# New step orders for the five engines of a batched attention kernel with adaptive normalization

## The chip, the cores and the metric

The kernel runs on one core of one Trainium2 chip. The metric is the device time of one launch in microseconds (us), as the median of several runs. A profile of one execution was taken beside the runs.

## The reference

```
scale, shift = split(emb @ W_emb + b_emb)              # emb: one row of 1024 for each batch
xn  = rms_norm(x, g_norm) * (1 + scale) + shift        # x: (8, 512, 1024)
q, k, v = xn @ W_qkv                                   # 16 heads of 64
q, k = rms_norm(q, g_q), rms_norm(k, g_k)
attn = softmax(q k^T * 64**-0.5)
o = attn @ v                                           # back to (8, 512, 1024)
out = x + o + o @ W_out
```

All data are float32.

## The kernel before

Every large product is made in two parts: an operand is split into a rounded high part (`_hi`, on ScalarE) and the rest (`_lo`, on VectorE or GpSimd), and TensorE multiplies high by high, high by low and low by high. The first two matmuls of a product keep the high part of the activations (L500, L501), the third has the low one (L502). The weights are split once, in the first batch, kept in `w_store` in HBM, and loaded again for each later batch.

The work is cut into *steps*, and each engine has its own written list of steps for the first batch (`HEAD`), for each of the six batches in the middle (`BODY`, run six times) and for the last one (`TAIL`). A step is written as pair of heads, letter, number: `7W0` is step W0 of pair 7. A batch has eight pairs. The lists run over the borders of a batch: a cycle of `BODY` begins with pair 2 of its own batch, and `8` and `9` are pairs 0 and 1 of the next. The letters, with the engines in the order in which the work passes them:

- **C** (TensorE, 4 for each of 4 tiles of 128 rows, six matmuls each): projection of q, k and v of a pair into `proj_bank`. **D** (ScalarE copies v and squares q and k, VectorE sums, GpSimd takes the root in two operations, L970 and L973) and **M** (VectorE, q and k scaled into `qk_stage`) drain the tile; two tiles later the bank is used again.
- **T** (TensorE turns q (T0) or k (T1) with four transposes into a `flip_bank`; ScalarE makes the high part, VectorE the low one).
- **S** (TensorE, scores of 128 queries by 512 keys into a `score_bank`; VectorE takes the maximum, L859; ScalarE the exponential with the row sum, L718). There are two score banks: S(n+2) waits for the exponential of S(n). **N** (VectorE): reciprocal of the row sum, L863, and the scaling of `probs`, L865, an operation with input and output in SBUF.
- **F** (TensorE turns 512 columns of `probs` with four transposes, L598, into one of two `flip_bank`s; ScalarE writes `pt_hi`, L724; VectorE `pt_lo`, L869, which frees the bank). **W** (TensorE, L609 and L610, product with v) needs both. F0 and F4 wait for the four N before them.
- **O** (ScalarE, VectorE: the two parts of the output added), **Q** (ScalarE `o_hi`, L734; GpSimd `o_lo`, L966, which reads and writes SBUF), **V** (ScalarE, GpSimd: parts of v), **P** (TensorE, output projection, 48 for a batch) and **R** (VectorE adds the residual, which a DMA brought).
- **A**, **X** (the next batch's x: square and scale, turn, modulate, split; the lows of X on GpSimd, L960), **L** (weights split in the first batch, on ScalarE, VectorE L767 and GpSimd L933), **B**.

Each engine runs its list strictly in order, and every step waits on semaphores for what it needs. So an order never changes what is computed, only who waits for whom. In `flip_places` and `flip_at` the places of T, F and X in TensorE's list say which of the two flip banks and which semaphore counts they use. The two waits that the prediction speaks of most:

```python
pe.wait_ge(exp_done, it * 8 + (n - 2 + 1 + CREDIT))                  # S
pe.wait_ge(flip_free, flip_at(order, b, "F", n, p)[0] + 1)           # W
```

Of the kernel before, what the change touches and what calls it, by code (L numbers as in the profile page):

```python
# [35 lines left out]
        X0 Z0 X1 0C0 0C1 0C2 X2 0C3 0C4 0C5 0C6 X3 0C7 0C8 0C9 0C10 0C11 0C12 0C13 0C14 0C15 1C0 1C1 1C2 1C3 0T0 0T1 1C4  # L36
        1C5 1C6 1C7 1C8 1C9 0S0 0S1 1C10 1C11 0S2 0S3 1C12 1C13 0S4 0S5 1C14 0F0 0F1 1C15 0S6 0S7 2C0 0F2 0F3 0W0 0W1
        2C1 2C2 0W2 2C3 0W3 1T0 1T1 2C4 2C5 2C6 2C7 0F4 2C8 2C9 0F5 1S0 0F6 0W4 1S1 2C10 0F7 0W5 1S2 1S3 0W6 2C11 0W7
        2C12 1S4 1S5 1F0 1F1 2C13 2C14 1F2 1W0 1F3 1W1 1S6 1S7 1W2 2C15 1W3 3C0 3C1 1F4 1F5 3C2 3C3 2T0 2T1 1W4 1W5 3C4
        3C5 3C6 1F6 3C7 3C8 1F7 1W6 2S0 2S1 3C9 3C10 1W7 2S2 3C11 3C12 2S3 2S4 3C13 3C14 3C15 2S5 2S6 4C0 2F0 2F1 4C1  # L40
        4C2 2S7 4C3 3T0 3T1 2W0 2W1 4C4 4C5 2F2 4C6 4C7 4C8 2F3 2W2 3S0 2F4 3S1 2F5 2W3 4C9 3S2 2F6 2W4 3S3 2F7 2W5 4C10
        2W6 4C11 2W7 3S4 3S5 4C12 3F0 3F1 4C13 3S6 4C14 3F2 3W0 3F3 3W1 3S7 4C15 3W2 5C0 3W3 3F4 3F5 5C1 5C2 3F6 3F7 3W4
        3W5 5C3 5C4 4T0 4T1 3W6 3W7 5C5 5C6 5C7 5C8 5C9 4S0 4S1 5C10 5C11 4S2 4S3 5C12 5C13 4S4 4S5 5C14 4F0 4F1 5C15
        4S6 4S7 6C0 4F2 4F3 4W0 4W1 6C1 6C2 5T0 4W2 5T1 4W3 6C3 6C4 6C5 4F4 6C6 6C7 6C8 4F5 5S0 4F6 4W4 5S1 6C9 4F7 4W5
# [40 lines left out]
        X1 1L0 1L1 1L2 X3 1L3 0D0 X5 0D1 X7 0D2 0D3 2L0 2L1 2L2 2L3 1D0 0V0 0V1 1D1 1D2 3L0 1D3 3L1 3L2 3L3 2D0 1V0 2D1
        1V1 2D2 0Q0 2D3 4L0 4L1 2V0 4L2 4L3 3D0 +A0 3D1 +A1 +A2 +A3 2V1 3D2 1Q0 5L0 3D3 5L1 5L2 5L3 4D0 4D1 3V0 3V1 4D2
        2Q0 6L0 4D3 6L1 6L2 6L3 4V0 5D0 4V1 5D1 3Q0 5D2 7L0 5D3 7L1 7L2 7L3 5V0 6D0 6D1 5V1 4Q0 6D2 6D3 6V0 7D0 +X0 +X1
        7D1 7D2 +X2 +X3 6V1 7D3 +X4 +X5 5Q0 8D0 +X6 +X7 8D1 8D2 7V0 7V1 8D3 L0 L1 L2 L3 6Q0 9D0 8V0 9D1 9D2 8V1 7Q0 9D3
        L4 L5 L6 L7 9V0 9V1 L8 L9 L10 L11""".split(),
# [1061 lines left out]
```

## Time and profile before

| | |
|---|---|
| median of 3 runs (lowest, highest) | 2278.11 us (2276.98, 2279.11) |
| profiled execution: its own time | 2278.89 us |
| profiled execution: span of its instructions | 2276.0 us |
| mean granted TensorE clock | 0.999 |
| TensorE, VectorE, ScalarE, GpSimd busy | 2256.2, 1597.9, 1345.7, 651.7 us |

The profile gives for each instruction the engine, the line, the start and the duration. TensorE's matmuls are pipelined: one is shown as lasting until its end is drained, while the next has begun. What a matmul costs TensorE is therefore the distance from its start to the next one's start, not its duration. TensorE can also be held up by less than the length of one matmul without an idle time being shown.

### The profile page before, as it was taken

The page shows a single profiled execution, that of the slowest core. Times are in us where ns is not written, and L with a number is a line of the kernel's source. Part 1 is how long each engine was busy: PE and PEld are TensorE (multiplying, and loading weights), DVE is VectorE, ACT ScalarE, POOL GpSimd, SP SyncE. Part 2 cuts the span into 40 slices and gives each one's busy share as a digit, 9 for nine tenths or more (in the row PEclk, how much of TensorE's full clock was granted, in tenths as well). Part 3 has the DMA queues.
Part 4 walks back from the last instruction along what each step waited for, and adds up shares of the span by engine and source line. Part 5 has one row for each costly group of instructions (what it writes and reads, how often), then busy time and mean ns, then how long its engine had stood idle before and what let it go on. Part 6 is the DMA issues. An engine that isn't in the chain of part 4 may idle for free.

```text
span 2276.0 us, 36733 instructions
## 1 busy us (share of the span) xinstructions
PE 2256.2 (99%) x13392; PEld 2110.3 (93%) x13392; DVE 1597.9 (70%) x3284; ACT 1345.7 (59%) x3101; POOL 651.7 (29%) x880
## 2 busy tenths in 40 slices
...
DMA packets 71269, 346.35 MB, mean 152 GB/s; under 512 B 7601, under 2 KB 43441, under 8 KB 47537
## 3 DMA queue, kind: packets, MB, share of 16 engines
...
## 4 chain that ended last, share of the span: by engine, by line
PE 86%; DVE 8%; ACT 2%; issue 1%; POOL 0%; DMA 0%; ACTq 0%; DVEq 0%
PE proj_bank L502 18%; PE proj_bank L500 18%; PE proj_bank L501 18%; PE flip_bank L598 9%; PE pv_bank L609 5%; PE pv_bank L610 5%; PE score_bank L590 4%; PE score_bank L591 4%; PE flip_bank L553 2%; DVE probs L865 2%; DVE neg_max L859 2%; DVE pt_lo L869 2%; PE flip_bank L563 1%; ACT k_hi L700 1%; PE proj_bank L525 1%
## 5 line engine op out<-in xcount | busy, mean ns | idle before, releaser
L500 PE MATMUL proj_bank<-w_split,xn_hi 128*128 128x384 f32 x2048 | 700.0, 342 | 1.4 <-DVE res L907 0.8
L502 PE MATMUL proj_bank<-w_split,xn_lo 128*128 128x384 f32 x2048 | 688.5, 336 | 0.0
L501 PE MATMUL proj_bank<-w_split,xn_hi 128*128 128x384 f32 x2048 | 687.4, 336 | 0.0
L718 ACT ACTIVATE probs<-score_bank,neg_max 128x512 f32<-128x512 f32 x512 | 352.6, 691 | 213.5 <-DVE neg_max L859 211.2
L500 PEld LDWEIGHTS proj_bank<-w_split,xn_hi 128*128 128x128 f32 x2048 | 385.2, 188 | 18.1 <-DVE xn_lo L854 1.0
L501 PEld LDWEIGHTS proj_bank<-w_split,xn_hi 128*128 128x128 f32 x2048 | 385.5, 188 | 15.2
L724 ACT CAST pt_hi<-flip_bank 128x512 fp32r<-128x512 f32 x512 | 288.8, 591 | 182.0 <-PE flip_bank L598 91.1
L869 DVE TENSOR_TENSOR pt_lo<-flip_bank,pt_hi 128x512 fp32r<-128x512 f32 x512 | 339.9, 685 | 78.1 <-ACT pt_hi L724 75.9
L502 PEld LDWEIGHTS proj_bank<-w_split,xn_lo 128*128 128x128 f32 x2048 | 384.8, 188 | 0.0
L859 DVE TENSOR_REDUCE neg_max<-score_bank 128x1 f32<-128x512 f32 x512 | 341.3, 684 | 17.0 <-PE score_bank L591 13.0
L865 DVE TENSOR_SCALAR probs<-probs,row_inv 128x512 f32<-128x512 f32 x512 | 275.7, 539 | 18.1
L598 PE MATMUL flip_bank<-ident,probs 128*128 128x128 f32 x2048 | 284.4, 273 | 1.1 <-DVE q_split L830 0.4
L598 PEld LDWEIGHTS flip_bank<-ident,probs 128*128 128x128 f32 x2048 | 242.5, 140 | 32.8 <-DVE pt_lo L869 7.3
L973 POOL TENSOR_TENSOR qk_rstd<-qk_ms_eps,neg_half 128x4 f32<-128x4 f32 x256 | 264.6, 1033 | 20.0
L970 POOL TENSOR_TENSOR qk_ms_eps<-qk_ms,eps_col 128x4 f32<-128x4 f32 x256 | 55.3, 216 | 719.2 <-DVE qk_ms L880 719.1
L609 PE MATMUL pv_bank<-pt_hi,v_split 128*128 128x512 f32 x512 | 224.3, 438 | 4.2 <-DVE pt_lo L869 4.2
L500 PE MATMUL proj_bank<-w_split,o_hi 128*128 128x384 f32 (+1 forms) x672 | 215.2, 320 | 0.0
L951 POOL TENSOR_TENSOR v_split<-v_stage,v_split 128x256 fp32r<-128x256 f32 x128 | 98.9, 773 | 401.3 <-ACT v_split L688 401.3
L502 PE MATMUL proj_bank<-w_split,o_lo 128*128 128x384 f32 (+1 forms) x672 | 213.6, 318 | 0.0
L501 PE MATMUL proj_bank<-w_split,o_hi 128*128 128x384 f32 (+1 forms) x672 | 213.5, 318 | 0.0
L590 PE MATMUL score_bank<-k_hi,q_split 128*128 128x512 f32 x512 | 206.0, 402 | 0.1
L591 PE MATMUL score_bank<-k_lo,q_split 128*128 128x512 f32 x512 | 201.6, 394 | 0.0
...
## 6 DMA issues: line engine op xcount, KB each, us to landing
...
```

Source lines behind the costliest of these rows:

```text
L500: nc.tensor.matmul(dst, a_hi, w_hi, start=(kt == 0), stop=False)
L501: nc.tensor.matmul(dst, a_hi, w_lo, start=False, stop=False)
L502: mm = nc.tensor.matmul(dst, a_lo, w_hi, start=False, stop=(kt == KT - 1))
L590: nc.tensor.matmul(score_bank[n % 2][:, :], q_t, k_hi[h][:, :], start=True, stop=False)
L591: nc.tensor.matmul(score_bank[n % 2][:, :], q_t, k_lo[h][:, :], start=False, stop=True).then_inc(score_full, 1)
L598: mm = nc.tensor.transpose(flip_bank[flip][:, qt * P:(qt + 1) * P], probs[h][:, qt, i * P:(i + 1) * P], ident[:, :])
L609: nc.tensor.matmul(pv_bank[h][:, :], v_t, pt_hi[n % 2][:, :], start=(i == 0), stop=False)
L718: nc.scalar.activation(probs[h][:, i, :], score_bank[n % 2][:, :], ACT.Exp, bias=neg_max[:, n:n + 1], accum_out=row_sum[:, n:n + 1]).then_ ...
L724: nc.scalar.copy(pt_hi[n % 2][:, :], flip_bank[flip][:, :]).then_inc(flip_hi, 1)
L859: nc.vector.tensor_reduce(neg_max[:, n:n + 1], score_bank[n % 2][:, :], AX.X, ALU.max, negate=True).then_inc(max_done, 1)
L865: nc.vector.tensor_scalar(probs[h][:, i, :], probs[h][:, i, :], row_inv[:, n:n + 1], None, ALU.mult).then_inc(probs_ready, 1)
L869: nc.vector.tensor_tensor(pt_lo[n % 2][:, :], flip_bank[flip][:, :], f32(pt_hi[n % 2][:, :]), ALU.subtract).then_inc(flip_free, 1)
```

## The change

It puts other step orders in the place of the old ones for all five engines, in `HEAD`, `BODY` and `TAIL`. Each list has the same steps as before. No function, wait, buffer or operation is edited. Of SyncE's lists only one pair of steps in `BODY` is exchanged (`E8 W4` becomes `W4 E8`); `HEAD` and `TAIL` have the same SyncE order as before. Shown are the lines of which the prediction speaks. The places of T, F and X in TensorE's list move, and with them the flip bank that a step uses.

```diff
--- before.py
+++ after.py
@@ -33,60 +33,60 @@
 HEAD = {
     "TensorE": """
...
-        7S1 6F3 6W1 6F4 6W2 8C12 7S2 6F5 6W3 7S3 6F6 6W4 8C13 6F7 6W5 7S4 6W6 8C14 8C15 6W7 7S5 7F0 7F1 7S6 9C0 9C1 7F2
-        8T0 7W0 7W1 7S7 9C2 9C3 8T1 7W2 9C4 7F3 9C5 9C6 9C7 8S0 8S1 7W3 9C8 7F4 7F5 9C9 8S2 9C10 8S3 9C11 7F6 7F7 7W4
...
+        6F5 7S0 7S1 6W4 8C10 6F6 6F7 6W5 7S2 8C11 7S3 +X3 6W6 6W7 7S4 7S5 7F0 7F1 7S6 7W0 7F2 7S7 7W1 7F3 8C12 8C13 7W2
+        7F4 7F5 7W3 8C14 7F6 7W4 7W5 7F7 8C15 9C0 7W6 9C1 7W7 8T0 9C2 9C3 8T1 9C4 9C5 9C6 9C7 8S0 8S1 9C8 9C9 8S2 8S3
...
     "VectorE": """
...
-        7N0 6F4 7N1 7S2 6F5 6O0 6F6 7N2 7S3 6F7 7S4 7N3 7N4 8D3 7S5 6O1 7F0 7F1 8M3 L0 7N5 L1 L2 L3 7F2 7S6 8T0 9D0 7S7
...
+        6F6 8D1 6F7 7S2 7S3 +X3 7N2 7S4 7N3 7S5 8M1 6O1 7F0 7N4 7F1 7S6 7N5 7S7 7F2 7N6 7N7 7F3 7F4 8D2 7F5 7F6 8M2 8D3
...
@@ -96,84 +96,84 @@
 BODY = {
     "TensorE": """
...
-        3F0 3F1 4C13 4C14 3F2 3W0 3F3 3W1 3S6 3S7 3W2 4C15 3W3 5C0 5C1 3F4 3F5 5C2 5C3 4T0 4T1 3W4 3W5 5C4 5C5 3F6 5C6
...
-        6F5 6W3 7S3 6F6 6W4 8C13 6F7 6W5 7S4 6W6 8C14 8C15 6W7 7S5 7F0 7F1 7S6 9C0 9C1 7F2 8T0 7W0 7W1 7S7 9C2 9C3 8T1
...
-        8S6 8F0 8F1 9C14 9C15 8F2 8F3 8W0 8W1 8S7 P0 8W2 8W3 9T0 9T1 P1 P2 P3 P4 8F4 P5 P6 8F5 8F6 8W4 9S0 9S1 8F7 8W5
...
+        3S6 3F0 2W6 2W7 4C15 3S7 3F1 5C0 5C1 3F2 3W0 3F3 3W1 5C2 3F4 3W2 3W3 5C3 3F5 3W4 4T0 5C4 4T1 5C5 5C6 5C7 3F6 5C8
...
+        7S3 +X3 6W6 7S4 6W7 7S5 8C10 8C11 7F0 7F1 7S6 7S7 7W0 7F2 7W1 7F3 8C12 8C13 8C14 8C15 7W2 9C0 7F4 7F5 7W3 9C1
+        7W4 7F6 7F7 7W5 9C2 8T0 9C3 9C4 7W6 8T1 9C5 7W7 9C6 9C7 9C8 9C9 8S0 8S1 9C10 9C11 8S2 8S3 9C12 9C13 9C14 8S4 8S5
+        8F0 9C15 8F1 P0 8S6 8S7 8W0 8F2 P1 8F3 8W1 9T0 P2 P3 9T1 P4 P5 8W2 P6 8F4 P7 8W3 8F5 8W4 8F6 9S0 9S1 P8 P9 P10
...
     "ScalarE": """
...
-        2F2 2F3 4D0 3T0 3V0 3T1 4D1 2F4 2O0 2F5 3S0 2F6 3S1 2F7 3S2 3S3 4D2 3V1 2O1 3F0 3S4 3F1 3S5 2Q0 3F2 3F3 3S6 4D3
...
+        4D0 3T0 3T1 2F4 +A3 3V0 4D1 3S0 3S1 2F5 2O0 1Q0 3S2 2F6 4D2 2F7 3S3 3S4 3S5 3S6 3V1 3F0 2O1 4D3 3F1 3S7 3F2 3F3
+        2Q0 3F4 3F5 5D0 4T0 4T1 5D1 3F6 3F7 4S0 4S1 4S2 4S3 5D2 4V0 3O0 4F0 4S4 4S5 4F1 5D3 3O1 4F2 4F3 4S6 4S7 4V1 4F4
...
     "VectorE": """
...
-        2F6 3N1 2F7 3S2 3S3 3N2 3N3 4D2 3S4 2O1 3S5 3F0 4M2 3F1 3N4 3N5 3F2 3S6 3F3 3S7 3N6 4D3 3N7 3O0 4M3 3F4 3F5 5D0
...
-        8N4 8S5 8S6 8F0 8F1 8N5 8N6 9D3 8F2 8F3 9M3 8S7 8N7 9T0 R0 9T1 8F4 8O0 8F5 9S0 8F6 9S1 9N0 R1 8F7 9N1 9S2 9S3
...
+        3S3 2F6 4D2 3N2 2F7 3S4 2O0 3N3 4M2 3S5 3S6 3N4 3N5 3F0 3S7 4D3 3F1 2O1 3N6 3N7 3F2 3F3 4M3 3F4 3F5 5D0 5M0 4T0
...
+        6F4 6O0 6F5 7S0 7S1 6F6 7N0 6F7 7S2 7S3 +X3 7S4 7N1 7N2 7N3 7S5 8D1 7F0 7F1 8M1 7S6 7S7 7F2 8D2 7N4 7N5 8M2 7N6
+        7N7 6O1 7F3 8D3 7F4 8M3 7F5 7F6 7F7 9D0 9M0 8T0 8T1 9D1 8S0 8S1 9M1 8N0 8S2 8S3 7O0 8N1 9D2 8N2 8N3 9M2 8S4 8S5
+        8F0 8N4 9D3 7O1 8F1 9M3 8F2 8S6 8S7 8F3 8N5 R0 8N6 9T0 8N7 9T1 8F4 R1 8F5 8F6 9S0 9N0 9S1 9S2 9S3 9N1 9N2 R2 8F7
...
     "GpSimd": """
-        0Q0 1Q0 2D0 2D1 2D2 2V0 2D3 2V1 3D0 3D1 +A0 +A1 3D2 +A2 +A3 3D3 4D0 3V0 4D1 3V1 4D2 2Q0 4D3 4V0 5D0 5D1 4V1 3Q0
-        5D2 5D3 5V0 6D0 6D1 5V1 4Q0 6D2 6D3 6V0 7D0 +X0 +X1 7D1 7D2 +X2 +X3 6V1 7D3 +X4 +X5 5Q0 8D0 +X6 +X7 8D1 8D2 7V0
-        7V1 8D3 6Q0 9D0 9D1 8V0 8V1 9D2 7Q0 9D3 9V0 9V1""".split(),
+        0Q0 2D0 2D1 2D2 2D3 3D0 3D1 3D2 2V0 2V1 +A0 +A1 +A2 3D3 4D0 4D1 1Q0 4D2 3V0 3V1 4D3 5D0 +A3 2Q0 5D1 4V0 5D2 5D3
+        4V1 6D0 6D1 3Q0 5V0 5V1 6D2 6D3 7D0 7D1 6V0 +X0 +X1 4Q0 7D2 +X2 6V1 +X3 7D3 8D0 +X4 +X5 5Q0 7V0 +X6 8D1 +X7 7V1
+        8D2 8D3 6Q0 9D0 9D1 8V0 9D2 9D3 7Q0 8V1 9V0 9V1""".split(),
     "SyncE": """
-        E2 E3 E4 3W1 E5 4W0 4W1 +X0 +X1 +X2 +X3 5W0 5W1 6W0 6W1 7W0 7W1 8W0 8W1 9W0 9W1 W0 W1 W2 W3 O0 E6 O1 E7 O2 E8 W4
+        E2 E3 E4 3W1 E5 4W0 4W1 +X0 +X1 +X2 +X3 5W0 5W1 6W0 6W1 7W0 7W1 8W0 8W1 9W0 9W1 W0 W1 W2 W3 O0 E6 O1 E7 O2 W4 E8
         W5 O3 E9 O4 E10 O5 E11 O6 10W0 +E0 10W1 O7 O8 O9 O10 11W0 +E1 O11""".split(),
 }
 
```

## Rows read from the trace of the kernel before

**Rows 1.** The page: busy time of each engine, share of the span, instructions

```profile
PE 2256.2 (99%) x13392; PEld 2110.3 (93%) x13392; DVE 1597.9 (70%) x3284; ACT 1345.7 (59%) x3101; POOL 651.7 (29%) x880
```

**Rows 2.** Busy time (count) in stretches, then the clock: first batch, a middle one

```profile
44.00:386.00 342.00, 338.03 (x2010) 316.30 (x2008) 274.73 (x549) 236.03 (x552) 138.33 (x166) 1.00 0.47 175
...
943.00:1222.00 279.00, 278.32 (x1671) 263.48 (x1670) 193.34 (x402) 163.33 (x376) 75.30 (x104) 1.00 0.39 144
```

**Rows 3.** Timeline, fourth batch, around 3W2: start, us, engine, line, [idle before]

```profile
1009.38 1.58 DVE L865 TENSOR_SCALAR probs<-probs,row_inv 128x512 f32<-128x512 f32 x1
1009.38 1.29 POOL L966 TENSOR_TENSOR o_lo<-o_pair,o_hi 128x512 fp32r<-128x512 f32 x1 [2.10 <-ACT o_hi L734]
...
1010.97 0.40 PE L590 MATMUL score_bank<-k_hi,q_split 128*128 128x512 f32 x1
1011.06 0.49 DVE L865 TENSOR_SCALAR probs<-probs,row_inv 128x512 f32<-128x512 f32 x1
1011.20 0.40 PE L591 MATMUL score_bank<-k_lo,q_split 128*128 128x512 f32 x1
1011.46 0.68 DVE L869 TENSOR_TENSOR pt_lo<-flip_bank,pt_hi 128x512 fp32r<-128x512 f32 x1
1012.06 0.68 DVE L859 TENSOR_REDUCE neg_max<-score_bank 128x1 f32<-128x512 f32 x1
1012.20 0.50 PE L609 MATMUL pv_bank<-pt_hi,v_split 128*128 128x512 f32 x1 [0.60 <-DVE pt_lo L869]
1012.53 0.39 PE L610 MATMUL pv_bank<-pt_lo,v_split 128*128 128x512 f32 x1
```

**Rows 4.** Timeline: the way of 3F4 and 3F5 with nothing queued

```profile
1016.38 1.03 PE L598 MATMUL flip_bank<-ident,probs 128*128 128x128 f32 x8
...
1017.01 1.08 ACT L724 CAST pt_hi<-flip_bank 128x512 fp32r<-128x512 f32 x2 [0.82 <-PE flip_bank L598]
1017.17 0.42 PE L500 MATMUL proj_bank<-w_split,xn_hi 128*128 128x384 f32 x1
...
1017.63 0.69 DVE L869 TENSOR_TENSOR pt_lo<-flip_bank,pt_hi 128x512 fp32r<-128x512 f32 x1 [0.39 <-ACT pt_hi L724]
```

**Rows 5.** Timeline, fourth batch, around 8F2

```profile
1155.12 1.02 DVE L865 TENSOR_SCALAR probs<-probs,row_inv 128x512 f32<-128x512 f32 x1
...
1157.56 0.34 PE L502 MATMUL proj_bank<-w_split,xn_lo 128*128 128x384 f32 x1
...
1157.98 1.25 PE L598 MATMUL flip_bank<-ident,probs 128*128 128x128 f32 x8
...
1158.99 0.47 PE L609 MATMUL pv_bank<-pt_hi,v_split 128*128 128x512 f32 x1
```

**Rows 6.** Timeline of TensorE, first batch, before 8T1

```profile
296.66 0.33 PE L501 MATMUL proj_bank<-w_split,xn_hi 128*128 128x384 f32 x1
296.83 0.34 PE L502 MATMUL proj_bank<-w_split,xn_lo 128*128 128x384 f32 x1
298.65 0.33 PE L553 MATMUL flip_bank<-ident,qk_stage 128*128 128x128 f32 x1 [1.48 <-DVE pt_lo L869]
```

**Rows 7.** Groups by line: VectorE's scaling of probs; count, busy us, mean ns, idle before

```profile
L865 DVE TENSOR_SCALAR probs<-probs,row_inv 128x512 f32<-128x512 f32 x512 | 275.7, 539 | 18.1
```

**Rows 8.** Timeline: an S step with nothing queued behind it

```profile
1151.06 0.40 PE L591 MATMUL score_bank<-k_lo,q_split 128*128 128x512 f32 x1
...
1151.50 0.69 DVE L859 TENSOR_REDUCE neg_max<-score_bank 128x1 f32<-128x512 f32 x1 [0.46 <-PE score_bank L591]
...
1152.81 0.19 ACT L718 ACTIVATION_READ_ACCUMULATOR probs<-score_bank,neg_max 128x1 f32 x1
```

**Rows 9.** Timeline: a T1 step on ScalarE and VectorE

```profile
1047.97 2.78 ACT L700 ACTIVATE k_hi<-flip_bank,gk_col 64x512 fp32r<-64x512 f32 x4
...
1050.78 1.51 DVE L834 SCALAR_TENSOR_TENSOR k_lo<-flip_bank,gk_col,k_hi 64x512 fp32r<-64x512 f32 x2 [1.49 <-ACT k_hi L700]
```

**Rows 10.** Groups by line: VectorE's part of X, four instructions a step

```profile
L796 DVE TENSOR_SCALAR y_half<-flip_bank,mod_now 128x128 f32<-128x128 f32 x128 | 43.7, 404 | 13.5 <-issue 8.2 <-PE flip_bank L563 4.4
```

More of the change, by code:

```diff
@@ L35 @@
     "TensorE": """
[L36 to L44, printed above, removed]
@@ L84 @@
-    "GpSimd": """
[L85 to L89, printed above, removed]
+        X0 Z0 X1 0C0 0C1 0C2 0C3 X2 0C4 0C5 0C6 0C7 X3 0C8 0C9 0C10 0C11 0C12 0C13 0C14 0C15 1C0 1C1 1C2 1C3 0T0 1C4 0T1
@@ new lines @@
+        1C5 1C6 1C7 1C8 1C9 0S0 1C10 0S1 1C11 0S2 1C12 0S3 1C13 1C14 1C15 0S4 0F0 0S5 0F1 2C0 2C1 0W0 0S6 0S7 0W1 0F2
+        0F3 2C2 2C3 1T0 1T1 2C4 2C5 0W2 2C6 2C7 2C8 0F4 0W3 1S0 0F5 1S1 2C9 0W4 1S2 0F6 1S3 0W5 0F7 2C10 2C11 1S4 0W6
+        0W7 2C12 1S5 1F0 1F1 2C13 2C14 2C15 1S6 1S7 1F2 1W0 1W1 3C0 1F3 3C1 3C2 2T0 3C3 2T1 1W2 3C4 3C5 1W3 3C6 1F4 3C7
+        2S0 2S1 1F5 3C8 3C9 1W4 1W5 2S2 1F6 1F7 3C10 3C11 2S3 1W6 3C12 2S4 3C13 2F0 2F1 1W7 2S5 3C14 3C15 4C0 2S6 2F2
+        2F3 2S7 2W0 2W1 4C1 4C2 3T0 4C3 3T1 4C4 2W2 4C5 2F4 2W3 4C6 4C7 2F5 2F6 3S0 3S1 2W4 2W5 2F7 4C8 4C9 3S2 3S3 4C10
@@ new lines @@
+        P22 9F0 9F1 P23 9S7 P24 P25 9W0 P26 P27 9F2 9F3 P28 P29 P30 9W1 P31 P32 P33 P34 P35 P36 P37 9F4 9W2 9W3 9F5 P38
+        P39 P40 9F6 P41 P42 9F7 9W4 9W5 P43 P44 P45 9W6 P46 9W7 P47""".split(),
+    "ScalarE": """
+        X0 Y0 Y1 1L0 1L1 X1 Y2 Y3 0D0 1L2 X2 Y4 Y5 1L3 0D1 X3 Y6 Y7 0D2 0D3 0V0 0V1 2L0 2L1 1D0 0T0 0T1 2L2 2L3 1D1 0S0
+        0S1 0S2 1D2 0S3 3L0 1D3 0F0 0F1 0S4 0S5 3L1 0S6 0F2 0F3 3L2 2D0 0S7 1T0 1T1 3L3 0F4 2D1 0F5 1S0 1S1 1S2 0F6 0F7
+        0O0 2D2 1S3 1S4 0O1 1F0 1F1 1V0 1V1 1S5 2D3 4L0 4L1 4L2 1F2 1F3 1S6 1S7 2T0 3D0 2T1 4L3 1O0 1F4 2V0 +A0 +A1 1F5
+        3D1 2S0 0Q0 2S1 1F6 1F7 3D2 2S2 2S3 +A2 +A3 2F0 2F1 1O1 2S4 2S5 2V1 3D3 5L0 5L1 5L2 5L3 2F2 2F3 2S6 2S7 3T0 3T1
+        2F4 4D0 3V0 1Q0 4D1 2F5 2O0 2F6 3S0 2F7 3S1 3S2 3S3 4D2 3V1 2O1 3F0 3S4 3S5 3F1 2Q0 3F2 3S6 3F3 3S7 4D3 3O0 4V0
+        3F4 3F5 6L0 6L1 3F6 4T0 6L2 5D0 4T1 5D1 3F7 4S0 4S1 4S2 4S3 6L3 5D2 4F0 4S4 4F1 3O1 4S5 4S6 4F2 4S7 4F3 4V1 5D3
+        7L0 7L1 7L2 4F4 7L3 4F5 6D0 5T0 5T1 4F6 6D1 3Q0 5V0 5S0 5S1 4F7 5S2 4O0 5S3 6D2 5S4 5F0 5F1 4O1 5V1 6D3 5S5 5F2
+        5F3 5S6 6T0 5S7 6T1 5F4 6V0 4Q0 7D0 7D1 5O0 +X0 5F5 6S0 6S1 5F6 5F7 6S2 6S3 +X1 6S4 6F0 6F1 5O1 7D2 7D3 6S5 6V1
+        6F2 6F3 6S6 5Q0 6S7 7V0 +X2 8D0 7T0 7T1 6F4 6O0 6F5 8D1 7S0 7S1 6F6 6F7 8D2 7S2 7S3 6O1 +X3 7F0 7S4 7F1 7S5 7F2
+        7S6 7S7 7F3 6Q0 7F4 7V1 7F5 7F6 7F7 7O0 8D3 L0 L1 8V0 L2 L3 8T0 9D0 8T1 8V1 7O1 9D1 8S0 8S1 8S2 8S3 8S4 8S5 7Q0
+        9D2 8F0 8F1 9D3 8S6 8S7 L4 8F2 8F3 8F4 8F5 L5 L6 9V0 9T0 9T1 8F6 8O0 L7 9S0 9S1 9S2 9S3 9S4 L8 L9 8F7 9S5 L10
+        L11 8O1 9V1 9F0 9F1 9S6 9S7 9F2 9F3 9F4 9F5 9F6 9F7 9O0 9O1""".split(),
```

169 lines of the change are left out of this document (81 added, 88 removed).

## The prediction, made before the change was run

> **What bounds the kernel now.** I read the page first. TensorE is busy 99% of the span, VectorE 70%, ScalarE 59% [rows 1], and its clock is full. A busy share can hide short waits, so I took stretches next: TensorE shows 4.0 us without a matmul in the 342 us of the first batch and 0.7 in the 279 of a middle one, both at clock 1.00 [rows 2]. Then the waits by name: what TensorE waits for is nearly always VectorE, late with `pt_lo` [rows 3]. As a matmul overlaps the next one, I read the real price of a wait in the timeline, from start to start.
>
> From those distances come the prices of a step. A matmul of S or W takes 0.23 us (1010.97 to 1011.20 [rows 3]), a step of two 0.46. Eight transposes and the drain behind them take 0.87 (1016.38 to 1017.17, and the next matmul 0.25 instead of 0.17 [rows 4]), so a step F or T takes 0.44, X twice that. A C step is six matmuls at 0.17 to 0.18 each (296.66 to 296.83 [rows 6]), 1.04 us. No list has a step more or less than before, so this work stays. What a new order can take away is waits alone.
>
> Adding up all distances that are longer than these prices gives some 20 us for the whole kernel. About 3 of them lie before 44 us, where x of the first batch is made ready; they stay. Some 7.5 lie in the first batch, 1.5 in each middle batch (9 in all), 0.3 in the last one. The largest of a middle batch are shown: before 3W2, where 1011.20 to 1012.20 is 1.00 instead of 0.23 and the next distance 0.33 instead of 0.23, so 0.87 lost [rows 3]; and before 8F2, where 1157.56 to 1157.98 is 0.42 instead of 0.17 and the eight transposes after it take 1.01 instead of 0.79, so 0.47 lost [rows 5]. The remaining 0.2, at 6F3 and 6S5, are of the same reading. The largest of the first batch is before 8T1: 296.83 to 298.65 is 1.82 instead of 0.17, 1.65 lost [rows 6].
>
> **The change part by part: what it removes.** Before 3W2 the reader sees why VectorE is late. Its scaling of 3N4 starts at 1009.38, together with GpSimd's `o_lo` of 2Q0, and takes 1.58 us where 0.49 is usual. All that follows, 3N5 and the `pt_lo` of 3F2, is 1.09 late [rows 3]. The line takes 275.7 us for its 512 [rows 7]; at 0.49 each it would be 251: 25 us of VectorE go to such meetings. 8N4 before 8F2 is another, 1.02 us [rows 5]. I looked at the stretch of each long one: a middle batch has six, 3N4, 5N2, 7N5 and 8N4 beside a Q, 6N0 and 6N2 beside the lows of x.
>
> The Trainium skill, page "SBUF — State Buffer", section "SBUF: two separate sides", says why: VectorE and GpSimd share a pair of ports, whichever instruction starts first holds it to its end, and the other is blocked; it counts operations of VectorE that use both read ports. The trace agrees: L865 waits, while `pt_lo`, which reads PSUM, keeps its 0.68 us. By that rule an N step beside a Q costs up to one Q, 1.29 us, more; with no rule at all I would only carry the 25 us over to the new lists, whatever their order.
>
> So I asked of each Q in the new `BODY` what stands beside it on VectorE. 2Q0 follows +A3 on GpSimd, and ScalarE makes its high part after 3F3: VectorE then has 4M3 3F4 3F5 5D0 5M0 4T0 4T1, no N. 6Q0 follows 8D3: 7F4 8M3 7F5 7F6 7F7, no N. 7Q0 follows 9D3 and 8F2: 8S6 8S7 8F3, then only 8N5. 1Q0 and 3Q0 begin behind both operations of the root of 4D1 and 6D1, by when 3N1, or 5N0 and 5N1, are done on VectorE. Only 4Q0 (6N0, 6N1), 5Q0 and the lows of x (6N4 to 6N7) can still meet an N, and the F that needs those N is 4 us or more off. The places themselves are looser too: from the end of 3F2 to 3W2 TensorE had W0 F3 W1 S6 S7 (2.28 us) and now has W0 F3 W1 5C2 3F4 (2.84); from 8F0 to 8F2 it had 2.52 and now has 3.90. I take the 1.5 us of a middle batch as removed: 6 x 1.54 = 9.2 us.
>
> In the first batch four weight splits (L0 to L3) stand among VectorE's steps ahead of 7F2, whose `pt_lo` frees the bank that 8T1 waited for [rows 6]. In the new list they stand behind 7F7. I take those 1.65 us as removed, and of the other 5.9 half, 2.9, as many more places of this kind are redrawn. That half is an estimate; its bounds are nothing and all.
>
> **What it adds.** The new lists are tight elsewhere. I took the shortest ways that a step can go with nothing queued. F to W: ScalarE starts 0.19 after the last transpose of F4 (16.38 + 0.44 = 16.82 to 17.01), VectorE 0.62 later and is done 0.69 after that, and 0.05 more for TensorE: 1.55 us [rows 4]. S to S(n+2): VectorE starts 0.21 after the step's end at 1151.29, ScalarE has its row sum at 1153.00; with the same 0.05, 1.76 us [rows 8]. T1 to S0: from ScalarE's start 1047.97 to VectorE's end 1052.29 is 4.32, with both hops 4.56 [rows 9]. Against them stand these distances on TensorE:
>
> In the new `BODY`, 7F0 to 7W0 has 7F1 7S6 7S7 between, 0.44 + 0.92 = 1.36: 0.2 us must be waited in each middle batch. 7F1 to 7W1 and 6W5 have 1.82, 7S4 has 1.79 against 1.76, so whatever is queued there is waited for. 3S0, 4S0 and 5S0 have 5.06 against 4.56. For the queues I take 0.3 per batch more, an estimate between nothing and the 1.09 of one N beside a Q. That is 6 x 0.5 = 3.0 us given back.
>
> In the new `HEAD` the stretch from 7S3 to 7F5 is overfull. VectorE has S3 to S7, X3, N2 to N7, 8M1, 6O1 and F0 to F3 to do before the bank for 7F5 is free. F takes 0.60 from start to start, 1011.46 to 1012.06, N the same (0.40 to the next start and some 0.2 for its reciprocal) [rows 3], and S too; five, six and four of them 9.0; X3 1.37, 43.7 by 32 [rows 10]; M and O 1.0; with the hops 11.6 us. TensorE has 9.3 us of work there. 2.3 us must be waited. 8T1 to 8S0 has 4.16 against 4.56, 0.4 more. Together 2.7.
>
> In the last batch nothing of size is found on either side. The exchange of W4 and E8 on SyncE moves one load by one issue and is hidden, as the weights are due a tile of P later; uncovered, it would cost TensorE at most that issue, below half a microsecond per batch.
>
> **The sum.** 9.2 - 3.0 in the middle batches, 1.65 + 2.9 - 2.7 in the first: 6.2 + 1.9 = 8.1 us. The profiled execution took 2278.9 us, its span 2276.0; the median of the runs is 0.8 lower than that execution. 2278.1 - 8.1 = 2270.0. I round to that.
>
> **The rivals.** *More is gained.* VectorE no longer loses its 25 us where they hurt, the tight places meet no queue, and the first batch loses most of its waits: 9.2 - 1.2 + 7.5 - 2.7 = 12.8, so 2265.3. At the extreme, all 17 us behind the start of the first batch go: 2261. For it speaks that the lists avoid the meetings almost one by one; against it, the overfull stretch in `HEAD`.
>
> *The waits only change place.* With the tight distances of pair 7, 6W4, 6W5 and 7S4 each as late as 8F2 was, a middle batch gives back 1.3 beside the 0.2, so 9.0 of the 9.2; with half of the first batch's 1.9 lost as well, 1.1 us are left: 2277. For it speaks that F to W falls from 2.25 us at the least to 1.36.
>
> *Slower.* One mechanism: VectorE in the stretch from 7S3 to 7F5 of every middle batch. If it is as overfull there as in `HEAD`, it makes TensorE wait 2.3 us a batch. By the same count the new `BODY` has 8C10, 8C11 and 6W7 more between S5 and F0, and a C behind F3, and is not overfull: S3, X3, S4, N1 to N3 end 4.6 us behind the end of 7S3, and 7F0 is due after 4.8. But if one N of it met the lows of x (1.3 us each, as long as the Q in [rows 3]) and the ScalarE queue were late by as much again, 2.6 to 3.5 us a batch would be lost: 6 x 3.5 = 21, less 11, gives 2288; it decides from 2.6 us a batch, where 15.7 less 11.1 is the 4.6 us that a measurement can tell.
>
> *Meetings are not avoided* (the change doesn't do what I read in it): the waits of 0.87 and 0.47 remain in another place beside the new ones: 9.2 less is taken off, 2279. Its chance is within that of the two cases before.
>
> **How the numbers follow.** Measurement tells 0.2%, 4.6 us, from no change. Forecast and the case of more gain together 0.70 (0.45 and 0.25), waits that change place 0.19, slower 0.11 with its milder half below 2283. The likeliest is 2270.0; its own range is 2266 to 2273. To hold 8 in 10, the range reaches to the better case at 2263 and through the case of no change to 2279.
>
> **What would show it.** In the profile after: 3W2 and 8F2 start without a gap, in all middle batches; L865 takes clearly less than 275.7 us, below 260; its long ones lie among 6N0 to 6N7; a wait of about 0.2 us before 7W0 in each middle batch; a wait of 2 us or so around 7F0 to 7F5 in the first. A middle batch becomes about 1 us shorter. The prediction is wrong if new waits of more than 1 us a batch stand at pair 6 or 7, or if TensorE's steps are themselves slower than the prices above.

## The result, and the profile after

The changed kernel takes 2288.94 us (median of 5 runs, 2288.39 to 2289.60), the kernel before 2278.11 beside it: ratio 1.0046, 95% interval 1.0031 to 1.0061. It is 0.46% slower, where 2270.0 had been forecast. The profiled execution took 2288.41 us, its span 2286.6, 10.6 more than before's.

The page of the changed kernel, busy times and the two groups that matter here (busy, mean ns of one, idle time before them and what ended most of it):

```profile
PE 2259.6 (99%) x13392; PEld 2108.8 (92%) x13392; DVE 1588.8 (69%) x3284; ACT 1347.8 (59%) x3101; POOL 648.8 (28%) x880
...
L598 PE MATMUL flip_bank<-ident,probs 128*128 128x128 f32 x2048 | 291.9, 273 | 11.2 <-DVE probs L865 10.3
...
L865 DVE TENSOR_SCALAR probs<-probs,row_inv 128x512 f32<-128x512 f32 x512 | 272.3, 532 | 18.2
```

Its waits of TensorE by name (us, times, longest):

```profile
PE flip_bank L598 <- DVE probs L865: 10.3, 13, 2.1
...
PE score_bank L590 <- ACT probs L718: 3.6, 7, 0.9
PE flip_bank L563 <- ACT y_half L660: 2.1, 1, 2.1
PE flip_bank L598 <- DVE pt_lo L869: 0.8, 1, 0.8
...
PE pv_bank L609 <- DVE pt_lo L869: 0.3, 1, 0.3
```

The waits for `pt_lo` [rows 3, 5] are gone from the middle batches (the two left are in the first), but TensorE now waits twice a batch for an N step (13 times with one in the first batch) and once for an exp (7 times, one of them in the first batch). The scaling N, L865, takes 272.3 us in all, against 275.7 [rows 7]: nearly as much is lost as before to what is called a meeting here, an N beside a long instruction of GpSimd. In a middle batch VectorE loses 2.9 us in four meetings (4N3, 6N0, 6N1, 7N2), before 3.5 in six; in the first batch 5.1 in nine, before 2.5 in six. From 6F0 of the 3rd batch (820.47) to 6F0 of the 4th (1100.50) are 280.03 us; before, from 3W2 to 3W2, 278.5. So a middle batch is 1.5 us longer, and six make 9 of the 10.8 us. Counting TensorE's matmuls along its lists gives the same by stage: `HEAD` takes 352.1 us instead of 350.4, the six cycles of `BODY` 1679.3 instead of 1670.4, `TAIL` 219.5 instead of 219.4. I read the 4th batch from start to start, as the prediction did. Its waits are 0.95 at 6F0, 0.75 at 7F0, 0.72 at 7S7, and the rest at 3F6, 8C4, 8C8, 6F5 and 7S3, each 0.1 to 0.24: some 3 us in all against 1.5.

**6F0.** VectorE's 6N0 and 6N1, GpSimd's second of two lows of x (+X1) and its 4Q0, and TensorE's last matmul of 6S5 and 6F0:

```profile
1093.54 1.40 DVE L865 TENSOR_SCALAR probs<-probs,row_inv 128x512 f32<-128x512 f32 x1
1094.86 0.15 DVE L863 RECIPROCAL row_inv<-row_sum 128x1 f32<-128x1 f32 x1
1095.05 1.32 DVE L865 TENSOR_SCALAR probs<-probs,row_inv 128x512 f32<-128x512 f32 x1
...
1092.11 2.54 POOL L960 TENSOR_TENSOR xn_lo<-y_half,xn_hi 128x512 fp32r<-128x512 f32 x2
1094.62 1.47 POOL L966 TENSOR_TENSOR o_lo<-o_pair,o_hi 128x512 fp32r<-128x512 f32 x1
...
1099.32 0.39 PE L591 MATMUL score_bank<-k_lo,q_split 128*128 128x512 f32 x1
1100.50 0.63 PE L598 MATMUL flip_bank<-ident,probs 128*128 128x128 f32 x4 [0.79 <-DVE probs L865]
```

Two steps of GpSimd back to back, and two N back to back beside them: 1.40 and 1.32 us instead of 0.49 each, 1.74 lost. Behind them VectorE has 7D2, 6S2, 6S3, +X1, 6N2 and 6N3 without a gap between them, and 6F0 needs 6N3. TensorE loses 0.95, 1100.50 less 1099.32 less the usual 0.23.

**7F0.** The same engines 26 us on: 7N2, GpSimd's +X6, TensorE's last matmul of 8C11, 7F0 with 7F1:

```profile
1127.02 1.32 DVE L865 TENSOR_SCALAR probs<-probs,row_inv 128x512 f32<-128x512 f32 x1
...
1126.50 1.55 POOL L960 TENSOR_TENSOR xn_lo<-y_half,xn_hi 128x512 fp32r<-128x512 f32 x1 [7.59 <-ACT xn_hi L666]
...
1128.16 0.34 PE L502 MATMUL proj_bank<-w_split,xn_lo 128*128 128x384 f32 x1
1129.08 1.07 PE L598 MATMUL flip_bank<-ident,probs 128*128 128x128 f32 x8 [0.58 <-DVE probs L865]
1129.90 0.48 PE L590 MATMUL score_bank<-k_hi,q_split 128*128 128x512 f32 x1
1130.21 0.40 PE L591 MATMUL score_bank<-k_lo,q_split 128*128 128x512 f32 x1
1131.06 0.50 PE L590 MATMUL score_bank<-k_hi,q_split 128*128 128x512 f32 x1 [0.45 <-ACT probs L718]
```

**7S7** is the last of these rows. It writes the bank that exp 7S5 frees, and ScalarE does 7F0 ahead of exp 7S5:

```profile
1129.74 0.58 ACT L724 CAST pt_hi<-flip_bank 128x512 fp32r<-128x512 f32 x1 [0.58 <-PE flip_bank L598]
1130.23 0.69 ACT L718 ACTIVATE probs<-score_bank,neg_max 128x512 f32<-128x512 f32 x1
1130.81 0.20 ACT L718 ACTIVATION_READ_ACCUMULATOR probs<-score_bank,neg_max 128x1 f32 x1
```

7F0's transposes end at 1129.08 + 0.44 = 1129.52. ScalarE starts 0.22 later, passes to the exp after 0.49 and ends it 0.78 later; 0.05 more and TensorE can go, 1.54 in all. TensorE has 7F1 and 7S6 to put there, 0.90. That is 0.64 short, whatever else the queue holds; 0.62 is lost before 7S7 and 0.10 behind its first matmul.

**HEAD.** Windows of the changed kernel, 2 us each (busy PE, PEld, DVE, ACT, POOL, granted clock, DMA):

```profile
283.00:285.00 2.00, 0.06 (x1) 0.00 (x0) 1.97 (x4) 1.97 (x6) 1.26 (x1) 1.00 0.00 0
285.00:287.00 2.00, 1.06 (x8) 0.85 (x8) 1.94 (x5) 1.62 (x5) 1.27 (x1) 0.81 0.00 0
287.00:289.00 2.00, 1.85 (x4) 1.39 (x5) 1.96 (x5) 1.25 (x5) 0.00 (x0) 0.50 0.00 0
289.00:291.00 2.00, 2.00 (x8) 1.78 (x7) 0.77 (x4) 0.88 (x2) 0.00 (x0) 0.50 0.00 0
291.00:293.00 2.00, 2.00 (x8) 1.70 (x8) 1.93 (x6) 1.48 (x5) 0.00 (x0) 0.50 0.00 0
293.00:295.00 2.00, 2.00 (x12) 2.00 (x12) 1.04 (x2) 0.78 (x2) 0.00 (x0) 0.98 0.00 0
```

8T1's 1.65 us [rows 6] are gone, but VectorE is full from 283 to 289, 7F0 starts 2.27 us late at 285.17 and 7S6 1.16 late at 287.15, and TensorE's granted clock is 0.50, its lower level of 1.2 GHz, until 293. From 287.15 to 293.25 the steps take 6.10 us; at their prices at full clock they would take 3.5, so some 2.6 us are lost (an estimate). 7F0 needs 7N3, and this is a meeting too, with a low of x:

```profile
283.64 1.38 DVE L865 TENSOR_SCALAR probs<-probs,row_inv 128x512 f32<-128x512 f32 x1
...
283.47 1.26 POOL L960 TENSOR_TENSOR xn_lo<-y_half,xn_hi 128x512 fp32r<-128x512 f32 x1 [2.98 <-ACT xn_hi L666]
```

### The profile page after: what moved, and what is told of

Read it like the earlier page. It is cut to its first block, busy times and chain, and to the rows that moved or that the text cites. A ratio compares the mean times of both kernels' runs of the same rounds, so it can differ in the third digit from the quotient of the medians.

```text
span 2286.6 us, 36733 instructions
## 1 busy us (share of the span) xinstructions
PE 2259.6 (99%) x13392; PEld 2108.8 (92%) x13392; DVE 1588.8 (69%) x3284; ACT 1347.8 (59%) x3101; POOL 648.8 (28%) x880
## 3 DMA queue, kind: packets, MB, share of 16 engines
q8 instruction: 106, 1.74, 0.3%
## 4 chain that ended last, share of the span: by engine, by line
PE 91%; DVE 6%; ACT 1%; issue 1%; POOL 0%; DMA 0%; SPq 0%; ACTq 0%; DVEq 0%
PE proj_bank L500 19%; PE proj_bank L502 19%; PE proj_bank L501 19%; PE flip_bank L598 9%; PE pv_bank L610 5%; PE pv_bank L609 5%; PE score_bank L590 4%; PE score_bank L591 4%; PE flip_bank L553 2%; DVE probs L865 2%; DVE neg_max L859 1%; DVE y_half L796 1%; PE proj_bank L621 1%; PE proj_bank L525 1%; PE proj_bank L526 1%
## 5 line engine op out<-in xcount | busy, mean ns | idle before, releaser
L724 ACT CAST pt_hi<-flip_bank 128x512 fp32r<-128x512 f32 x512 | 298.1, 588 | 388.3 <-PE flip_bank L598 258.6
L869 DVE TENSOR_TENSOR pt_lo<-flip_bank,pt_hi 128x512 fp32r<-128x512 f32 x512 | 350.4, 688 | 192.3 <-ACT pt_hi L724 187.1
L718 ACT ACTIVATE probs<-score_bank,neg_max 128x512 f32<-128x512 f32 x512 | 350.7, 691 | 222.2 <-DVE neg_max L859 219.4
L598 PE MATMUL flip_bank<-ident,probs 128*128 128x128 f32 x2048 | 291.9, 273 | 11.2 <-DVE probs L865 10.3
L865 DVE TENSOR_SCALAR probs<-probs,row_inv 128x512 f32<-128x512 f32 x512 | 272.3, 532 | 18.2
L609 PE MATMUL pv_bank<-pt_hi,v_split 128*128 128x512 f32 x512 | 217.7, 425 | 0.3 <-DVE pt_lo L869 0.3
```

The costliest lines, as they stand in the source:

```text
L598: mm = nc.tensor.transpose(flip_bank[flip][:, qt * P:(qt + 1) * P], probs[h][:, qt, i * P:(i + 1) * P], ident[:, :])
L609: nc.tensor.matmul(pv_bank[h][:, :], v_t, pt_hi[n % 2][:, :], start=(i == 0), stop=False)
L718: nc.scalar.activation(probs[h][:, i, :], score_bank[n % 2][:, :], ACT.Exp, bias=neg_max[:, n:n + 1], accum_out=row_sum[:, n:n + 1]).then_ ...
L724: nc.scalar.copy(pt_hi[n % 2][:, :], flip_bank[flip][:, :]).then_inc(flip_hi, 1)
L865: nc.vector.tensor_scalar(probs[h][:, i, :], probs[h][:, i, :], row_inv[:, n:n + 1], None, ALU.mult).then_inc(probs_ready, 1)
L869: nc.vector.tensor_tensor(pt_lo[n % 2][:, :], flip_bank[flip][:, :], f32(pt_hi[n % 2][:, :]), ALU.subtract).then_inc(flip_free, 1)
```

## The experiments

All times are medians, ratios are to the kernel before, run beside each (2277.94 to 2278.79).

**1 and 2. Both kernels with the meetings taken away.** The low halves that GpSimd makes shrink to a sliver in the middle batches: 4 of 512 columns of `o_lo`, 1 of 128 of `xn_lo`, 1 of 64 of V. Their outputs are therefore not the reference's. Shown is the edit for `o_lo`; those for X and V are of the same kind.

```diff
-                        nc.gpsimd.tensor_tensor(o_lo[:, p % PAIRS, :], o_pair[:, :], f32(o_hi[:, p % PAIRS, :]),
+                        k = 4 if order is BODY else T
+                        nc.gpsimd.tensor_tensor(o_lo[:, p % PAIRS, 0:k], o_pair[:, 0:k], f32(o_hi[:, p % PAIRS, 0:k]),
```

> The new orders, with GpSimd's low parts in the middle batches cut to a sliver: o_lo to 4 of 512 columns, the lows of x and v to 1 column of 128 or 64. What is left out is that part of the low-order terms of those batches. Steps, waits and orders are kept. Theory A (in each middle batch VectorE's 6N0, 6N1 and 7N2 meet a long GpSimd instruction, each is some 0.85 us longer, and TensorE waits 0.94 us before 6F0 and 0.74 before 7F0): both waits go, 6 x 1.68 = 10 us, 2279 or somewhat below. Theory B (the new orders are too tight for VectorE and ScalarE as such, whatever GpSimd does): 2286 or more, with the waits before 6F0 and 7F0 still there.

> The old orders with the same cut of GpSimd's low parts in the middle batches, and so the same part left out. Theory A: the waits before 3W2 (0.87 us) and 8F2 (0.47) go, 6 x 1.34 = 8 us, 2270; and then the kernel is to be compared with the new orders under the same cut: if the meetings were the whole difference of the middle batches, both are left with waits of less than 1.3 us a batch. Theory B: 2276 or more.

The new orders took 2279.15 (1.0005, 0.9996 to 1.0013), the old ones 2269.75 (0.9963, 0.9949 to 0.9978). So taking the meetings out of the middle batches gains the new orders 9.8 us and the old ones 8.4 (9.6 and 8.2 against the kernel before run beside them). The cut also lets GpSimd's results come sooner; experiments 4, 10 and 11 leave nothing out and agree. That meetings are the larger part of the new waits in the middle batches is shown, and L865 falls to 254.8 us. That they are the difference of the two kernels is refuted: 9.4 us stay between them without any, 7.9 of it in the middle batches (`BODY` 1669.3 and 1661.4 us). With clean N steps, the new orders show how much cover 6F0 has (VectorE's 6N3, the last matmul of 6S5, 6F0):

```profile
1096.23 0.49 DVE L865 TENSOR_SCALAR probs<-probs,row_inv 128x512 f32<-128x512 f32 x1
...
1097.22 0.39 PE L591 MATMUL score_bank<-k_lo,q_split 128*128 128x512 f32 x1
1097.45 0.60 PE L598 MATMUL flip_bank<-ident,probs 128*128 128x128 f32 x4
```

6N3 ends at 1096.72, and 6F0 starts at 1097.45 without a wait: 0.73 us of cover. 1.74 lost less 0.73, with 0.05 to pass it on, is 1.06, close to the 0.95 seen.

**3. The HEAD of before with the new BODY and TAIL.**

```diff
-HEAD = { the new lists }
+HEAD = { the lists of before }
```

> The first batch's order of the kernel before, with the new orders of the middle batches and the last. Theory A puts 9 of the 10.8 us into the middle batches, so this is only 2 to 3 us faster than the new kernel: 2286.5. Theory C (the loss is the first batch's, through the overfull stretch of 7F0 to 7F3 and the half clock behind it): 2280 or less.

2287.23 (1.0040, 1.0027 to 1.0053), 1.7 less than the new kernel. The two intervals overlap, so by the times alone this is not clear of noise; the traces agree with it, with `HEAD` 1.7 us longer in the new kernel. The new HEAD then gives back all that 8T1 gave, and 1.7 more; the other 9 us lie in BODY, as `TAIL` differs by 0.1.

**4. The new BODY with GpSimd's two steps out of the way.**

```diff
 BODY["GpSimd"]
-... 7D0 7D1 6V0 +X0 +X1 4Q0 7D2 ... 7V0 +X6 8D1 +X7 ...
+... 4Q0 7D0 7D1 6V0 +X0 +X1 7D2 ... 7V0 8D1 +X6 +X7 ...
```

> The new kernel with two steps of GpSimd's list for the middle batches moved: 4Q0 ahead of 7D0, so that it is over before 6N1, and +X6 behind 8D1, so that it is not beside 7N2. Nothing is left out. Theory A: 6N1 and 7N2 return to 0.49 us, the waits before 6F0 and 7F0 (0.94 and 0.74 us) go; the wait before 7S7 (0.72) stays, as it hangs on ScalarE, whose X3 is 2.7 us long; 6 x 1.7 = 10 us, so 2279. Theory B: no gain of more than 2 us, 2287 or more.

2281.43 (1.0014, 1.0005 to 1.0024), 7.5 less. 6F0 waits 0.1 and 7F0 not at all; 7S7 keeps 0.69, and 8C12 waits 0.29 for the low of x that now comes later. Two steps of an engine that is busy 28% of the span make most of the new waits: 1.6 of some 3 us a batch.

**5. What is left at 7S7: ScalarE's X?** Experiment 1, and ScalarE's scalings and roundings of X on 1 column of 128 in the middle batches, so that more of the output is wrong.

> The new orders with GpSimd's low halves of Q, X and V cut to a sliver in the middle batches, as in the earlier run of that kind, and ScalarE's part of X (four scalings and two roundings of 512 elements a row) cut to 1 column of 128 as well; both leave the output of the middle batches wrong in part. That earlier run took 2279.15 and had 1.4 us of waits a middle batch left: 7S7 0.70, 6F5 0.29, 8C4 0.24, 7S3 0.10, 7S6 0.09. If they are ScalarE's queue, which the new order of it makes late with +X3 ahead of 7S4 and +X2 ahead of 8D0, they go nearly all: 2271 to 2273. Rival: they are VectorE's chain of S and N, or the matmuls' own order; then within 1 us of 2279.

2276.74 (0.9992, 0.9984 to 1.0001), 2.4 less: 6F5 and 7S6 lost their waits, 0.38 a batch. 7S7 kept 0.62 and 0.11. Here ScalarE stood idle ahead of 7F0 (ScalarE, then TensorE):

```profile
1124.48 0.59 ACT L728 CAST pt_hi<-flip_bank 128x512 fp32r<-128x512 f32 x1 [1.10 <-PE flip_bank L598]
1124.97 0.69 ACT L722 ACTIVATE probs<-score_bank,neg_max 128x512 f32<-128x512 f32 x1
...
1125.80 0.50 PE L590 MATMUL score_bank<-k_hi,q_split 128*128 128x512 f32 x1 [0.45 <-ACT probs L722]
```

So the theory that +X3 ahead of 7S4 makes 7S7 wait fell. What is left fits the shortage of 0.64 worked out above: 7F0, then exp 7S5, in a place of 0.90 us.

**6. Then exp 7S5 first.**

```diff
 BODY["ScalarE"]
-... 7S4 7F0 7S5 7F1 ...
+... 7S4 7S5 7F0 7F1 ...
```

> The new orders with one step moved: ScalarE's 7S5 of BODY ahead of 7F0. The run without ScalarE's X still had 0.62 us of wait at 7S7 and 0.11 behind it, with ScalarE idle ahead of 7F0, so +X3 ahead of 7S4 isn't what makes 7S7 wait. If it is that exp 7S5 stands behind 7F0, whose matmuls come 0.7 us late for another reason, exp 7S5 starts 0.6 us earlier and 7S7's wait goes nearly whole: 3.5 to 4.3 us less in six batches, about 2285. Rival: 7S5's maximum on VectorE is as late, and 7S7 waits all the same: within 1 us of 2289.

2288.95 (1.0046, 1.0033 to 1.0059): nothing. 7S7 has its bank in time, and 7W0 waits instead:

```profile
1131.85 0.40 PE L591 MATMUL score_bank<-k_lo,q_split 128*128 128x512 f32 x1
1132.80 0.47 PE L609 MATMUL pv_bank<-pt_hi,v_split 128*128 128x512 f32 x1 [0.56 <-DVE pt_lo L869]
```

0.95 instead of 0.23: 0.72 lost, and 0.08 behind it, against 0.72 at 7S7. Of the two things that ScalarE owes TensorE here, one is late in either order. More work of TensorE between 7F0 and 7W0 should cover it (before, 9C0, 9C1, 7F2 and 8T0 stood there); that was not tried.

**7 and 8. HEAD.** First VectorE's 7N3 ahead of 7S4, ScalarE's 7S4 ahead of 7F0 and 6O1 behind +X3; then, on TensorE alone, projections into the two gaps.

```diff
 HEAD["VectorE"]
-... 7N2 7S4 7N3 7S5 ...
+... 7N2 7N3 7S4 7S5 ...
 HEAD["ScalarE"]
-... 7S3 6O1 +X3 7F0 7S4 7F1 ...
+... 7S3 +X3 6O1 7S4 7F0 7F1 ...
```

> The new orders with three steps of HEAD moved: VectorE's 7N3 ahead of 7S4, ScalarE's 7S4 ahead of 7F0 and its 6O1 behind +X3. BODY and TAIL stay. If 7F0's wait of 2.3 us and 7S6's of 1.4 are these queues, and the fall of TensorE's granted clock to 0.50 from 287 to 293 us follows from them, the first shrinks to about 1.5, the second to under 0.8, and the clock may stay up: 1.5 to 5 us less, about 2286. Rival: 7F0 waits for ScalarE's +X3 whatever stands around it and the clock falls all the same: within 1 us of 2289.

```diff
 HEAD["TensorE"]
-... 7S5 7F0 7F1 7S6 ... 7F3 8C12 8C13 7W2 ...
+... 7S5 8C12 7F0 7F1 8C13 7S6 ... 7F3 7W2 ...
```

> The new orders with two steps of HEAD moved on TensorE alone: 8C12 from behind 7F3 to ahead of 7F0, and 8C13 to ahead of 7S6, so that 2.1 us of projections stand in the two long waits (2.27 at 7F0, 1.16 and 0.28 at 7S6). If the waits are an order that puts too little between +X3 and 7S6, they fall to 1.1 and to nearly nothing; and if the fall of TensorE's granted clock to 0.50 between 287 and 293 us follows from these waits, it goes too. Together 2 us without the clock's part and 5 with it: 2284 to 2287. Rival: the work of the projections is only moved, the places behind 7F3 then wait, and the clock falls all the same: within 1 us of 2289.

The first took 2288.63 (1.0046, 1.0032 to 1.0060). 7N3 starts 0.09 us ahead of the low of x there and takes 0.49 us, while the low takes 1.53 instead of 1.26; so who starts first decides who loses. 7F0's wait fell from 2.27 to 0.78, 7S6's rose from 1.16 to 1.65, and the clock was 0.61 and 0.54 for 4 us. `HEAD` is 1.2 us shorter in its trace (350.8 for 352.1), but the median is within the noise of the new kernel's. The second took 2290.79 (1.0053, 1.0039 to 1.0067), 1.9 more:

```profile
284.16 0.39 PE L591 MATMUL score_bank<-k_lo,q_split 128*128 128x512 f32 x1
288.34 0.69 PE L500 MATMUL proj_bank<-w_split,xn_hi 128*128 128x384 f32 x1 [3.79 <-POOL xn_lo L960]
```

8C12 reads the last low of x, which GpSimd has only at 288.29. The C steps that could fill the gap hang on the same chain, and the clock fell to 0.50 again (289 to 291 us).

**9. Five of these moves together** (experiments 4, 6 and 8).

> The new orders with five steps moved: GpSimd's 4Q0 and +X6 of BODY as in the earlier run with these two (2281.43), ScalarE's 7S5 of BODY ahead of 7F0, and 8C12 and 8C13 of HEAD on TensorE. If the parts add up (7S5 4 us, HEAD 2 to 5), the time is 2273 to 2276, below the 2278 of the kernel before. Rival: with +X6 out of the way 7F0 comes in time, so that 7S5 has no wait left to give: 2277 to 2279.

2283.79 (1.0021, 1.0012 to 1.0030), above both the forecast and its rival, and 2.4 above experiment 4, about what 8C12 costs in HEAD. 7S7 waits 0.21 and 7W0 0.80. So moving 7S5 gains nothing without the meeting of 7N2 either, but not for the rival's reason: the wait is still there, at 7W0.

**10 and 11. The old orders, with their two meetings moved.** First ScalarE's 2Q0 ahead of 3S4, so that GpSimd's 2Q0 is done before 3N4; then also GpSimd's 7Q0 behind 9D3.

```diff
 BODY["ScalarE"]
-... 2O1 3F0 3S4 3F1 3S5 2Q0 3F2 ...
+... 2O1 3F0 2Q0 3S4 3F1 3S5 3F2 ...
 BODY["GpSimd"]
-... 9D2 7Q0 9D3 9V0 9V1
+... 9D2 9D3 7Q0 9V0 9V1
```

> The kernel before with one step moved: ScalarE's 2Q0 of BODY stands ahead of 3S4 instead of behind 3S5, so that GpSimd's low half of 2Q0 runs ahead of VectorE's 3N4 and not beside it. If the wait at 3W2 (0.78 us and 0.11 at the matmul behind it, in each of the 6 middle batches) is that meeting and nothing else, 3N4 takes 0.68 us, the wait goes and the time falls by 5.2 us, to about 2272.7. Rival: the wait is 3F2's and 3F3's place behind exp on ScalarE, or comes back elsewhere; then the time stays within 1 us of 2278.

> The kernel before with two steps moved: 2Q0 as in the run with one step moved, and GpSimd's 7Q0 of BODY behind 9D3, so that it isn't beside VectorE's 8N4. If 8F2's wait (0.3 us and 0.2 at the matmuls behind it, a batch) is that meeting, another 2.8 us go: about 2270. Rival: 7Q0 now meets 8N7 and the store of the wait moves to 9T0 or later; then as the kernel with one step moved, about 2272.7.

2273.28 (0.9977, 0.9968 to 0.9985) and 2270.91 (0.9967, 0.9955 to 0.9980). The waits at 3W2 and 8F2 are gone, each for one moved step. This is the fastest version that leaves nothing out, 18.0 us below the changed kernel. GpSimd's 2Q0 and VectorE's 3N4 in it:

```profile
1005.41 1.29 POOL L966 TENSOR_TENSOR o_lo<-o_pair,o_hi 128x512 fp32r<-128x512 f32 x1 [0.35 <-ACT o_hi L734]
...
1007.32 0.48 DVE L865 TENSOR_SCALAR probs<-probs,row_inv 128x512 f32<-128x512 f32 x1
```

**12. And 9C4 and 9C5 ahead of 8T1 in HEAD.**

```diff
 HEAD["TensorE"]
-... 9C3 8T1 7W2 9C4 7F3 9C5 9C6 ...
+... 9C3 9C4 9C5 8T1 7W2 7F3 9C6 ...
```

> The kernel before with the two steps 2Q0 and 7Q0 moved as in the earlier run (2270.91), and on TensorE in HEAD 9C4 and 9C5 ahead of 8T1, where 1.65 us of wait stand. If projections can stand in that wait, 8T1 comes 0.5 us later than now and 1 to 1.5 us are gained: about 2269.7. Rival: 8S0 and the steps behind it wait for the later 8T1, or a bank isn't free for 9C4: within 0.5 us of 2271.

2271.06 (0.9966, 0.9953 to 0.9978), no gain. 8T1 has no wait any more; 7F3 has 0.81 and 8S0 1.27 instead of 0.14 and 0.24: the 1.65 us have moved.

## Why the prediction was wrong

- **The balance.** `BODY` in the traces gives the terms of the six middle batches: 8.9 us taken off (experiment 2), 10.0 put back by meetings (experiment 1), where the prediction had nothing, and 7.9 by the tight places, where it had 3.0. That is 9.0 longer, where 6.2 shorter was forecast; the first batch adds 1.7.
- **The removals were right.** 3W2 and 8F2 start without a gap, and 8T1's 1.65 us are gone. The prices 0.87 and 0.47 a batch, 5.2 and 2.8 us in six, are nearly what single moves gain by themselves: 5.0 and 2.4 (experiments 10 and 11).
- **The step that failed** is "Only 4Q0 (6N0, 6N1), 5Q0 and the lows of x (6N4 to 6N7) can still meet an N, and the F that needs those N is 4 us or more off". The place of the meeting was named rightly, and the distance too: 6N1 ends at 1096.37 and 6F0 starts at 1100.50. But the cover was not worked out along VectorE's queue, which has no gap between the two: 0.73 us of cover was there, not 4. Two meetings in a row cost 1.74. That is 0.95 a batch, 5.7 us. The rule behind it held. The Trainium skill, page "SBUF — State Buffer", section "SBUF: two separate sides", says that of two such instructions the one that starts later is blocked until the other has ended. The trace agrees: 6N0 ends 0.29 us behind +X1, 6N1 0.28 behind 4Q0 and 7N2 0.29 behind +X6, each a little less than the 0.49 that an N takes alone.
- **The stretch behind 7S3.** The slower rival had it: 4.6 us against 4.8, and one N beside the lows of x. That meeting is there in each middle batch, 7N2 beside +X6, 0.83 us longer, and costs 0.75, 4.5 us in six. The prediction's list left out 7N2 (and 4N3, which meets a V, takes 0.83 us and makes nothing wait); that the rival got only 0.11 may have followed from that list. The rival gave 2288, the right time with the wrong sum, and so by luck: 3.5 us a batch were to be lost in this stretch, and it lost 1.5, with 0.95 at 6F0 ahead of it; the rest was made up by small waits and by the first batch, which was to gain 1.9.
- **Mis-sized: the tight places.** They were taken at 0.2 for 7F0 to 7W0 and 0.3 for queues, from ways "with nothing queued". 7F0 and exp 7S5 share ScalarE in a place of 0.90 us. Measured 0.72, in one order at 7S7, in the other at 7W0. Small ones at 8C4, 8C8, 6F5, 7S3 and 3F6 add more than the 0.3.
- **The first batch.** The overfull stretch was named rightly. That 2.3 was forecast and 2.27 measured at 7F0 is luck: the 2.3 were for the whole stretch and held no meeting, while 7N3 alone was 0.89 longer by one, and the stretch has 1.16 more at 7S6. What was not in the sum at all is some 2.6 us at the lower clock. Forecast a gain of 1.9, measured a loss of 1.7. Of the other waits behind 44 us, those over 0.12 us add up to 3.3 before and 1.6 after: 1.7 less, where 2.9 were taken.
- **In its own signs:** L865 was to fall below 260 us and stayed at 272.3; of the four long ones of a middle batch two lie among 6N0 to 6N7; a middle batch was to be 1 us shorter and is 1.5 longer. "New waits of more than 1 us a batch", named as what would make it wrong, stand at pairs 6 and 7.

Open: which instructions make 8C4, 8C8 and 3F6 late, some 0.6 us a batch, was not tried, nor was `HEAD` without its nine meetings.
